# Selective scan of a small sequence model: B kept in PSUM, C broadcast by DMA, three buffers, and dB*x as fp32 products in 64-row tiles

## What is computed

```python
xp = jnp.einsum('bld,rd->blr', x, x_proj_w)
dt_in, B, C = xp[..., :16], xp[..., 16:32], xp[..., 32:]
dt = jax.nn.softplus(jnp.einsum('blr,dr->bld', dt_in, dt_proj_w) + dt_proj_b)
dA = jnp.exp(dt[..., None] * A)                          # A = -exp(A_log), 512 x 16
dBx = dt[..., None] * B[:, :, None, :] * x[..., None]
def step(h, inp):
    dA_t, dBx_t, C_t = inp
    h = dA_t * h + dBx_t
    y = jnp.einsum('bdn,bn->bd', h, C_t)
    return (h, y)
_, ys = jax.lax.scan(step, h0, (dA, dBx, C))             # over the 1024 tokens
y = jnp.moveaxis(ys, 0, 1) + D * x
```

## Time and profile before

| | |
|---|---|
| median of 3 runs | 1026.04 us (1024.95 to 1766.46) |
| the profiled execution, its own time | 1026.57 us |
| its span, from the first instruction to the last | 1024.5 us |
| busy in the span | PE 892.6 us, DVE 708.2 us, ACT 417.1 us, POOL 261.4 us |
| mean clock granted to TensorE | 0.929 of full |
| first scan of step 0 starts, last scan ends | 33.72 us, 263.05 us after the span's start |

### The profile page before, as it was taken

The page is one execution under the profiler, slowest core; times in us unless marked ns, Lnnn a source line. Parts: engine busy times, 40 slices in busy tenths (PEclk is TensorE's granted clock), DMA queues, the critical chain, the costliest instruction groups (busy, mean ns, idle before and its releaser), DMA issues.

```text
span 1024.5 us, 20305 instructions
## 1 busy us (share of the span) xinstructions
PE 892.6 (87%) x8113; PEld 422.3 (41%) x8128; DVE 708.2 (69%) x906; ACT 417.1 (41%) x495; POOL 261.4 (26%) x149
## 2 busy tenths in 40 slices
PE   6466768668689999999979999999998899999997
PEld 1322334334344444445533444444443444444443
DVE  5899899998766334444678777777874497887243
ACT  3633545443234321144424555555655723324100
POOL 0343678797411001044520000000000122233000
PEclk8665789998789999999989999999998999999998
DMA  4000000000422000000010000000002111431001
GB/s 163 1 2 1 2 2 3 3 3 3 144 93 80 0 0 1 1 4 6 9 26 1 22 23 12 11 21 21 11 12 101 51 51 50 140 110 50 1 31 52
DMA packets 22759, 33.67 MB, mean 33 GB/s; under 512 B 8210, under 2 KB 15250, under 8 KB 22691
## 3 DMA queue, kind: packets, MB, share of 16 engines
q1 hardware_dynamic: 22690, 32.67, 10.1%
HBM read 26.30 MB, written 2.10 MB: 28 GB/s over the span
## 4 chain that ended last, share of the span: by engine, by line
PE 67%; DVE 20%; POOL 5%; issue 3%; ACT 3%; DMA 1%; SPq 1%; POOLq 0%; DVEq 0%; ACTq 0%
PE ps L809 11%; PE ps L598 9%; PE ps L576 7%; DVE arena L1182 7%; PE ps L656 7%; PE ps L717 7%; PE ps L705 6%; PE ps L836 6%; PE ps L622 5%; POOL arena L1049 5%; DVE arena L1150 3%; DVE arena L1326 2%; PE ps L460 2%; PE ps L637 1%; PE ps L659 1%
## 5 line engine op out<-in xcount | busy, mean ns | idle before, releaser
L1326 DVE TENSOR_REDUCE arena<-ps 128x1 f32<-128x512 f32 (+3 forms) x304 | 190.4, 659 | 50.0 <-PE ps L659 31.2
L995 ACT ACTIVATE arena<-ps 128x1024 f32<-128x1024 f32 (+4 forms) x192 | 147.1, 811 | 131.9 <-PE ps L705 98.2
L1049 POOL TENSOR_TENSOR arena<-arena 128x1024 f32<-128x1024 f32 x64 | 159.7, 2505 | 105.5 <-DVE arena L1182 104.5
L1182 DVE TENSOR_TENSOR_SCAN arena<-arena,ps 128x1024 f32<-128x1024 f32 x64 | 145.4, 2280 | 13.9 <-POOL arena L1049 5.9
L893 ACT ACTIVATE arena<-arena,negA 128x1024 f32<-128x1024 f32 x64 | 73.6, 1150 | 118.1 <-DVE arena L1182 115.7
L656 PE MATMUL ps<-arena 128*128 128x512 f16 (+3 forms) x384 | 112.6, 336 | 9.3 <-DVE arena L1326 5.9
L809 PE MATMUL ps<-arena 128*128 128x512 f16 x528 | 114.3, 379 | 1.6 <-DVE arena L1260 1.6
L705 PE MATMUL ps<-arena 128*128 (+4 forms) x384 | 103.8, 331 | 6.5 <-ACT arena L995 3.6
L490 PE MATMUL ps<-arena 64*128 64x64 f16 x3072 | 65.1, 202 | 44.3 <-DVE arena L1182 40.9
L490 PEld LDWEIGHTS ps<-arena 64*128 64x128 f16 x3072 | 57.0, 103 | 111.1 <-DVE arena L1182 91.9
L598 PE MATMUL ps<-arena 128*128 128x512 f16 x448 | 97.4, 380 | 1.6 <-DVE arena L1260 1.6
(11 more groups left out here) (133 smaller groups left out, 1080.4 us busy)
## 6 DMA issues: line engine op xcount, KB each, us to landing
arena<-in_w_q_dram SPq DMA_DIRECT2D x11, 768.0 KB, 4.4
arena<-in_w_s_dram SPq DMA_DIRECT2D x11, 384.0 KB, 4.7
arena<-arena SPq DMA_DIRECT2D x28, 128.0 KB, 2.4
arena<-in_x_fm_dram SPq DMA_DIRECT2D x4, 512.0 KB, 5.2
out_dram<-arena SPq DMA_DIRECT2D x8, 256.0 KB, 2.0
arena<-in_wg_dram SPq DMA_DIRECT2D x1, 1792.0 KB, 9.2
arena<-in_wu_dram SPq DMA_DIRECT2D x1, 1792.0 KB, 7.5
arena<-in_wd_dram SPq DMA_DIRECT2D x1, 1792.0 KB, 7.4
```

Of the source, the lines that this page charges most:

```text
L995: nc.scalar.activation(dst, src, ACT.Exp, scale=float(HD) ** -0.5).then_inc(exp_done, 1)
L1049: nc.gpsimd.tensor_tensor(hC[u][:], hst[:, u % 2, :], c_all[:, n, :], ALU.mult).then_inc(hc_done, 1)
L1182: nc.vector.tensor_tensor_scan(hst[:, i % 2, :], dA[:, i % 2, :], banks(2 * (i % 2), 2), 0.0, ALU.mult, ALU.add).then_inc(scan_done, 1)
L1326: nc.vector.reduce_max(dst, ps[:, n % 2, 0:len(slices) * w].rearrange("p (a w) -> p a w", a=len(slices)), AX).then_inc(ring_read, 1)
```

## The change

Parts of the change, all in the scan block:

1. B. DVE copies the 16 rows of B out of PSUM itself, PE turns them into bank 4, and they stay there as fp32 until the last diagonal is built. A diagonal is one fp32 instruction (L1118 of the changed kernel) from the 64x64 identity in SBUF and B in PSUM. Six are built before the first scan, and one behind each of the first ten. The first `dt_linear` writes banks 0 and 1 in place of 4 and 5.
2. dB*x. Both factors are fp32: one product a block in place of three, 8 x 2 = 16 matmuls a step. The turned dt*x needs one copy, on ACT (`keep_tok`); `tok_low` is gone.
3. C. ACT copies the 32 rows of B and C to SBUF, SP stores the 16 rows of C to DRAM, waits for that, and issues 16 DMAs, each of which broadcasts one row to 128 partitions. POOL's product waits for the DMA of its row in chunk 0. `bcast`, its copies on ACT, the selection matrix and the splitting in three parts are gone.
4. Buffers. dA and h have three buffers in place of two, so that ACT waits for the scan of step i-3 and the scan for POOL's product of step i-3. The PSUM pairs of dB*x stay two. POOL's steps are written out in place of a loop.
5. Loads. SP's load of the up weights of the next block waits for POOL's last product in place of the last `make_dbx`. In chunk 0, ACT's parts of `soft_log` for chunk 1 come one step earlier.

The diff, cut to its core:

```diff
-DT_BANK = (4, 6, 4, 4)
+DT_BANK = (0, 6, 4, 4)
...
-        dtx_tok = [view(kb, 2 * T, f16).rearrange("p (s q d) -> p s q d", s=2, q=TT) for kb in (36, 40)]
-        diag = [view(kb, 2 * TT * SUB, f16).rearrange("p (s q t) -> p s q t", s=2, q=TT)
+        dtx_tok = [view(kb, T, f32).rearrange("p (q d) -> p q d", q=TT) for kb in (36, 40)]
+        diag = [view(kb, TT * SUB, f32).rearrange("p (q t) -> p q t", q=TT)
...
+            sp.wait_ge(rows_kept, 1)
+            sp.dma_start(c_dram, bc_rows[NS:2 * NS, :]).then_inc(c_stored, 16)
+            sp.wait_ge(c_stored, 16)
+            for n in range(NS):
+                sp.dma_start(c_all[:, n, :], c_dram[n:n + 1, :].broadcast_to([P, T])).then_inc(c_loaded[n], 16)
+            sp.wait_ge(hc_done, DC * NS)
-            sp.wait_ge(dbx_done, DC * NS)
             sp.dma_start(wu0_sb[:], wu0.rearrange("(c p) m -> p c m", p=P)).then_inc(ld_w0, 16)
...
                 if n == 0:
-                    pe.wait_ge(tok_low_done, c + 1)
+                    pe.wait_ge(tok_kept, c + 1)
                 for q in range(TT):
-                    for k, (s, e) in enumerate(((0, 0), (0, 1), (1, 0))):
-                        for r in range(2):
-                            rows = slice(SUB * r, SUB * r + SUB)
-                            last = nc.tensor.matmul(ps[:, 2 * (i % 2) + r, q * SUB:(q + 1) * SUB], dtx_tok[c % 2][rows, s, q, :],
-                                                    diag[n][rows, e, q, :], start=(k == 0), stop=(k == 2))
+                    for r in range(2):
+                        rows = slice(SUB * r, SUB * r + SUB)
+                        last = nc.tensor.matmul(ps[:, 2 * (i % 2) + r, q * SUB:(q + 1) * SUB], dtx_tok[c % 2][rows, q, :],
+                                                diag[n][rows, q, :], start=True, stop=True)
                 last.then_inc(dbx_done, 1)
...
-                    if c == 0 and n + 1 < NS:
-                        pe.wait_ge(c_kept, n + 1)
-                        bcast(n + 1)
...
-                    if i >= 2:
-                        act.wait_ge(scan_done, i - 1)
-                    nc.scalar.activation(dA[:, i % 2, :], dt_[:, c % 2, :], ACT.Exp, scale=negA[:, c, n:n + 1]).then_inc(dA_done, 1)
-                    if c == 0:
-                        act.wait_ge(c_bcast, n + 1)
-                        nc.scalar.copy(c_all[:, n, :], banks(4, 2)).then_inc(c_kept, 1)
+                    if i >= 3:
+                        act.wait_ge(scan_done, i - 2)
+                    nc.scalar.activation(dA[i % 3][:], dt_[:, c % 2, :], ACT.Exp, scale=negA[:, c, n:n + 1]).then_inc(dA_done, 1)
...
-                nc.vector.tensor_tensor(diag[n][:, 0], mask64, b_tok[:, 0, :, n:n + 1].broadcast_to([P, TT, SUB]), ALU.mult)
-                nc.vector.tensor_tensor(diag[n][:, 1], mask64, b_tok[:, 1, :, n:n + 1].broadcast_to([P, TT, SUB]),
-                                        ALU.mult).then_inc(diag_built, 1)
+                nc.vector.tensor_tensor(diag[n][:], mask64, b_all[:, :, n:n + 1].broadcast_to([P, TT, SUB]), ALU.mult).then_inc(diag_built, 1)
...
-                if i >= 2:
-                    dve.wait_ge(hc_done, i - 1)
-                nc.vector.tensor_tensor_scan(hst[:, i % 2, :], dA[:, i % 2, :], banks(2 * (i % 2), 2), 0.0, ALU.mult, ALU.add).then_inc(scan_done, 1)
+                if i >= 3:
+                    dve.wait_ge(hc_done, i - 2)
+                nc.vector.tensor_tensor_scan(hst[i % 3][:], dA[i % 3][:], banks(2 * (i % 2), 2), 0.0, ALU.mult, ALU.add).then_inc(scan_done, 1)
...
-            build_diag(0)
-            build_diag(1)
+            for n in range(3):
+                build_diag(n)
             for part in range(4):
                 make_dt(0, part)
-            build_diag(2)
-            tok_low(0)
+            for n in range(3, 6):
+                build_diag(n)
```

More of the change, by code:

```diff
@@ L123, in build @@
         fold_sb = small("fold_sb", [P, 2 * NS])
+        ident64 = small("ident64", [P, SUB])
+        c_dram = nc.dram_tensor("c_rows", [NS, T], f32, kind="Internal").ap()
         alog_sb = small("alog_sb", [P, DC, NS])
@@ L321, in build @@
         ld_wraw = [sem(f"ld_wraw{w}") for w in range(4)]
-        sel_built, consts_made = sem("sel_built"), sem("consts_made")
-        xp_done, bc_split, dtin_done, negA_done = sem("xp_done"), sem("bc_split"), sem("dtin_done"), sem("negA_done")
+        fold_used, consts_made = sem("fold_used"), sem("consts_made")
+        xp_done, dtin_done, negA_done = sem("xp_done"), sem("dtin_done"), sem("negA_done")
         dtl_done, z_abs, softlog, dt_done = sem("dtl_done"), sem("z_abs"), sem("softlog"), sem("dt_done")
[L325 to L330, removed]
+        rows_kept, c_stored = sem("rows_kept"), sem("c_stored")
+        c_loaded = [sem(f"c_loaded{n}") for n in range(NS)]
+        b_kept, b_turned, diag_built, ident64_made = (
+            sem("b_kept"), sem("b_turned"), sem("diag_built"), sem("ident64_made"))
+        z_pos, dtx_done, dtx_turned, tok_kept = (
+            sem("z_pos"), sem("dtx_done"), sem("dtx_turned"), sem("tok_kept"))
         dA_done, dbx_done, scan_done, hc_done = sem("dA_done"), sem("dbx_done"), sem("scan_done"), sem("hc_done")
@@ L447, in dt_linear @@
                 last.then_inc(dtl_done, 1)
[L449 to L454, removed]
             def add_y(slot, start, stop):
@@ L466, in turn_rows @@
                 for q in range(TT):
-                    last = nc.tensor.transpose(ps[:, 0, q * NS:(q + 1) * NS], b_rows[0:NS, q * P:(q + 1) * P], ident_sb[0:NS, 0:NS])
+                    last = nc.tensor.transpose(ps[:, 4, q * NS:(q + 1) * NS], b_rows[0:NS, q * P:(q + 1) * P], ident_sb[0:NS, 0:NS])
                 last.then_inc(b_turned, 1)
@@ L524, in _ @@
                                 pe.wait_ge(z_pos, 2)
+                                pe.wait_ge(z_abs, 2)
                         add_y(i % 4, n == LAG, n == LAG - 1)
@@ L877, in soft_log, with keep_tok @@
                     nc.scalar.activation(dtx[:], banks(DT_BANK[c], 2), ACT.Relu).then_inc(z_pos, 1)
-            def tok_high(c):
+            def keep_tok(c):
                 act.wait_ge(dtx_turned, c + 1)
-                nc.scalar.copy(dtx_tok[c % 2][:, 0].rearrange("p q d -> p (q d)"), banks(TURN_BANK[c], 2)).then_inc(tok_high_done, 1)
+                nc.scalar.copy(dtx_tok[c % 2][:].rearrange("p q d -> p (q d)"), banks(TURN_BANK[c], 2)).then_inc(tok_kept, 1)
             for part in range(4):
@@ L899, in _ @@
                     if c == 0 and n == 0:
-                        tok_high(0)
+                        keep_tok(0)
                         soft_log(1, 3)
-                    if c + 1 < DC and 2 <= n < (5 if c == 0 else 6):
-                        soft_log(c + 1, (0, 1, 2)[n - 2] if c == 0 else (0, 3, 1, 2)[n - 2])
+                    if c == 0 and 1 <= n < 4:
+                        soft_log(1, n - 1)
+                    elif c and c + 1 < DC and 2 <= n < 6:
+                        soft_log(c + 1, (0, 3, 1, 2)[n - 2])
                     if c + 1 < DC and n == (NS - 1 if c == 0 else 11):
-                        tok_high(c + 1)
+                        keep_tok(c + 1)
             def norm_stage(ln, turn=True):
@@ L1041, in _ @@
             for c in range(DC):
-                def step(n, u, first):
+                for n in range(NS):
                     i = n + NS * c
@@ L1045, in step @@
                     if c == 0:
-                        pool.wait_ge(c_kept, n + 1)
-                    if not first:
+                        pool.wait_ge(c_loaded[n], 16)
+                    if i >= 4:
                         pool.wait_ge(y_added, i - 3)
-                    nc.gpsimd.tensor_tensor(hC[u][:], hst[:, u % 2, :], c_all[:, n, :], ALU.mult).then_inc(hc_done, 1)
-                for n in range(4):
-                    step(n, n, c == 0)
-                with pool.Fori(1, NS // 4) as k:
-                    for u in range(4):
-                        step(4 * k + u, u, False)
+                    nc.gpsimd.tensor_tensor(hC[i % 4][:], hst[i % 3][:], c_all[:, n, :], ALU.mult).then_inc(hc_done, 1)
             def keep(ln):
@@ L1203, in _ @@
                 for n in range(NS):
-                    if c + 1 < DC and n == (NS - 1 if c == 0 else 13):
-                        tok_low(c + 1)
                     scan(n, c)
@@ L1208, in _ @@
                         take_y(c - 1)
-                    if c == 0 and n + 3 < NS:
-                        build_diag(n + 3)
+                    if c == 0 and n + 6 < NS:
+                        build_diag(n + 6)
                     if c + 1 < DC and 6 <= n < 10:
```

50 lines of the change are left out of this document (13 added, 37 removed).

## The result

The changed kernel takes 1124.29 us (1122.16 to 1126.27, 4 runs) against 1026.32 us before: a ratio of 1.096, 95% interval 1.092 to 1.100. It is slower by 98 us, outside the range of 982 to 1072. One of the four executions of the kernel before took 1766.46 us and is left out of the ratio.

The account below looks back on a forecast made before the run. PE was taken to pace the scan block, its clock in between. First scan at 34.4, chunk 0 61.8 us and the others 164.0 end the block at 260.2, not 263.0: 2.8 us gained, forecast 1024, range 982 to 1072.

Parts of the forecast that it names:

- The step of PE: Scan block: `make_dbx` 1.81 us plus `add_y` 1.03 make 2.85 us a step at full clock, 5.4 at half.
- 3.8 us: Alternative step of PE at half clock, if the skill's load time of 107 ns held there too, in place of 5.4.
- hidden loads: Rival: loads in `make_dbx` cost nothing, DVE (2.85 us) and POOL (2.4) pace, kernel 983 us; chance 0.14.
- tiles in turn: Rival: the two row tiles of `make_dbx` load one after another, 4.5 us a step, kernel 1095 us; chance 0.04.
- I take 40% of the time in chunk 0 ... and 15% in chunks 1 to 3 as now: Assumed shares of half clock on PE, giving mean steps of 3.51 us in chunk 0 and 3.07 behind it.
- PE paces at half clock: Rival: `make_dbx` with `add_y` mostly at half clock, 2.55 us more a step, kernel over 1046 us; chance 0.20.
- half clock throughout: Extreme of the half-clock rival: every step of PE in the scan block at half clock, kernel 1154 us.
- B in PSUM: DVE's diagonal as one fp32 instruction: 0.6 us, not held by POOL, so DVE's step in chunk 0 is 2.8 us, not 5.54.
- The front: Before the first scan: turning dt*x starts at 27.70, 1.4 us gained and given back by `make_dbx`, first scan at 34.4.
- C and the buffers: C by DMA 0 us (0 to 30 if loads did not overlap), third buffer 0, earlier activations 0, up weights 0.
- The third buffer: Third buffer of dA and h: removes DVE's waits for POOL that PE's pace would cover anyway, worth 0.
- The steps with `make_dt`: Four steps of chunk 0: 4.1 us each at full clock, 5.4 at half, 4.5 on average, 18.2 together.

Follow-up runs that it names:

- e2_tiles64: Changed kernel with each fp32 product cut in two of 64 features, in four 64x64 tiles: 981.00 us, ratio 0.956 to the kernel before.
- e1_wide: Changed kernel with products of 128 columns in place of 64, same loads and results: 1010.09 us, ratio 0.985 to the kernel before.
- e7_tiles_bsbuf: The e2_tiles64 kernel with B copied to SBUF, so that a diagonal reads two SBUF operands: 983.59 us, ratio 0.959 to the kernel before.
- e8_tiles_swap: The e2_tiles64 kernel with DVE's part of `make_dt` ahead of the diagonal in steps 6 to 9 of chunk 0: 970.74 us, ratio 0.948.
- e4_fp32_alone: Kernel before with one fp32 diagonal from B in SBUF and one product a block, B, C and two buffers as before: 1088.64 us, ratio 1.062.

## Why the prediction was wrong

**The step of PE was right.** It said 2.85 us at full clock and 5.4 at half; measured 2.95 and 5.52. The time from `make_dbx` to `add_y` is 1.93 and 3.60 us where 1.81 and 3.50 were worked out, and the loads took 182 ns at least and 330 in the middle of all, as the earlier trace rows had it from L445. At half clock a step did not take the 3.8 us that the prediction set beside its 5.4. The rivals with hidden loads and with tiles in turn fell. By the Trainium skill ("TensorE: Matmul & The Clock Gate", section "Weight-path perf modes — Fast Weight Load (FWL) and DoubleRow") fp32 weights get no fast load; the traces agree, with 182 ns for the shortest fp32 load of 64x128 and 92 for the f16 one. What loads of 128 columns cost over those of 64 e2_tiles64 shows: 1.0 us a step at full clock.

**The step that failed is "I take 40% of the time in chunk 0 ... and 15% in chunks 1 to 3 as now".** Measured, the grants of 0.51, 0.62, 0.53 and 0.50 are half clock for 98%, 76%, 94% and all of the time. The rival "PE paces at half clock" was the right one; the forecast put 0.20 on it and cut the range at 1072 for 75%. By the prediction's own terms 75% of half clock throughout gives some 1090 to 1098 us and not 1072, so the top of the range was also set too low for what it was said to cover. Its price for half clock throughout, 1154, is 30 us above what came, for two things that it left out, some 28 us together: the first four steps have no `add_y` yet (3.4 us each in place of 5.5), and full clock held for two `make_dbx` at the start of chunk 1 and for six around that of chunk 2. With the measured shares in place of 40% and 15%, the prediction's terms put the end of the block at about 367 us, and it came at 366.6. That it fits so closely is luck, since the first four steps are priced too high by 8 us and the step and the front too low by about as much; but it shows that the share of half clock is the term that failed. The reason against it, that PE now has almost no gap, took a busy PE for a streaming one: PE was busy in 100% of the block, and by the prediction's own prices (0.056 us for a product, 0.104 for its load) the array waited for loads in half of `make_dbx`. The same text named this ("the array streams for only half the time") and gave it no weight. In the kernel before, chunks 1 to 3 had idle gaps on PE and yet 0.93; e1_wide settles it, since it changes the columns streamed and written and nothing else. What halves and restores the clock at one moment and not at another is not settled.

**B in PSUM.** 0.6 us start to start was right (0.66 each, the next instruction 0.58 behind). The reason was half right: e7_tiles_bsbuf shows that one instruction with two SBUF operands isn't held either, as long as it starts ahead of POOL. The rule of the Trainium skill ("SBUF — State Buffer", section "Who interferes with whom") also says that issue order decides which of the two blocks. It agrees with e7 in that POOL's product, which started second, was the one lengthened, and with e8_tiles_swap, where an instruction with one SBUF operand ran beside POOL in 0.69 us.

**The front.** First scan at 35.94, forecast 34.4: the turning started at 28.96 in place of 27.70, and the rest was as worked out within 0.3 us. In e1_wide, whose front is the same, the first `make_dbx` started at 29.75 and not at 32.12, so a miss of this size lies within what the front varies by.

**C and the buffers.** C cost nothing, as taken: POOL never waited for a DMA. The rows took longer to land than the 4.7 to 6.3 us of the estimate: 10.1 us in the median, with all 16 issued between 19.5 and 29.2 us. From 56 us on the page shows 1 to 2 GB/s, and POOL took the last row at 114:

```profile
arena<-c_rows SPq DMA_DIRECT2D x16, 512.0 KB, 10.1
```

The third buffer was nothing under PE's pace, as taken: e4_fp32_alone, with two buffers, has the same steps of 2.95 and 5.52 us. It is worth 4 to 8 us where PE does not pace.

**The steps with `make_dt`** in chunk 0 cost 5.7 to 5.9 us where 4.1 to 5.4 were taken: behind the diagonal, `make_dt` started after POOL and took 3.0 us. The row for that was in the trace before, as the second half of the diagonal.

## What to carry to other kernels

A product with few columns and a full 128-column fp32 weight is paced by its load (here 64 columns: 1.93 us for 16 products at full clock), and a busy PE then does not stream all the time. Price such a part at half clock throughout as one end of the range; the changed kernel had it for 92% of the block. Cut the weights into column tiles so that a load is about as short as its product, or give the product more columns: both brought the clock back here, to a grant of 0.96 and of 0.97 to 1.00 behind chunk 0. On DVE, put the instruction with two SBUF operands first behind the one that releases GpSimd, and the one with an operand in PSUM after it.

## What the runs showed that was not expected

- Useless work on PE made the kernel faster: nearly twice the streamed columns took 114 us off, and 8 us of turnings took 54 us off.
- Both clocks persisted through the same load-bound steps, 5.52 us or 2.95 us each: half clock for 30 `make_dbx` in a row, full clock for 14. Short events stood where it changed (a turning of 1.97 us with `add_y` up; a `dt_linear` with 17 rows, or a wait of 1.5 to 2.5 us, down), and not every one changed it.
- The same work on PE in chunks 1 to 3 took 220.9 us in one kernel and 250.7 in another; both began chunks 1 and 2 at full clock, and one lost it sooner.
